# A graph network's sorted messages: ScalarE places the kept edge ends at fixed places, VectorE's selection steps read them without register loads

## The reference

```python
x = x + L0_gnn(layernorm(x), edge_index, edge_attr, u, batch, W1, b1, W2, b2)   # mean of edge_attr by src, two-layer MLP
x = x + L0_ffn(layernorm(x)[None], ...)[0]                                      # two experts of eight, GELU, layer norm
x = x + L1_gnn(layernorm(x), W, edge_index)
x = x + L1_ffn(layernorm(x)[None], ...)[0]                                      # one expert per token, capacity 977

def L1_gnn(x, W, edge_index):
    src, dst = edge_index
    h = x @ W
    deg = segment_sum(ones_like(dst), dst)
    deg_inv_sqrt = where(deg > 0, rsqrt(maximum(deg, 1)), 0.0)
    norm = deg_inv_sqrt[src] * deg_inv_sqrt[dst]
    return segment_sum(h[src] * norm[:, None], dst)
```

## Time and profile before

| what | value |
|---|---|
| median of 3 runs | 3174.09 us (3173.44 to 3176.77) |
| the profiled execution | 3175.92 us, its span 3174.1 us |
| TensorE (PE) | 2284.6 us busy, 72% |
| VectorE (DVE) | 2044.1 us busy, 64% |
| GpSimd (POOL) | 2067.8 us busy, 65% |
| ScalarE (ACT) | 863.4 us busy, 27% |
| granted TensorE clock, mean | 0.826 |
| the chain that ended last | PE 35%, POOL 25%, issue 15%, DVE 13% |

### The profile page before, as it was taken

How to read it: one execution, slowest core, us unless ns; L and a number is a source line. 1 busy time by engine, 2 the same in 40 slices (tenths; PEclk the granted TensorE clock), 3 DMA queues, 4 the chain that set the end, 5 groups by cost and what they waited for, 6 DMA issues and landing times.

```text
span 3174.1 us, 49123 instructions
## 1 busy us (share of the span) xinstructions
PE 2284.6 (72%) x14349; PEld 2096.1 (66%) x14350; DVE 2044.1 (64%) x3305; ACT 863.4 (27%) x2246; POOL 2067.8 (65%) x1707
## 2 busy tenths in 40 slices
PE   0000047779899995997889984777887877798997
PEld 0000036668888885775889873666676767798997
DVE  8889976732323332465788876765665567488987
ACT  0000012210000000132545442344454421354543
POOL 5777877777777775010555545567788742488886
PEclk9999998865555555698999996899999895699999
DMA  6543345455444452122011114566777753423231
GB/s 202 151 115 94 81 124 152 146 163 123 114 114 117 113 136 71 50 77 66 20 49 51 51 61 139 140 165 187 193 197 190 192 146 112 86 63 84 63 90 33
DMA packets 341517, 358.60 MB, mean 113 GB/s; under 512 B 209280, under 2 KB 248560, under 8 KB 341125
## 3 DMA queue, kind: packets, MB, share of 16 engines
q1 hardware_dynamic: 209538, 196.84, 21.3%
q0 software_dynamic: 105984, 93.52, 13.0%
q10 hardware_dynamic: 25853, 66.46, 6.8%
HBM read 234.90 MB, written 122.85 MB: 113 GB/s over the span
## 4 chain that ended last, share of the span: by engine, by line
PE 35%; POOL 25%; issue 15%; DVE 13%; DMA 4%; DVEq 4%; SPq 4%; ACT 1%; another core or an unknown queue 0%; POOLq 0%; ACTq 0%
POOL sorted L989 18%; PE ps L1984 13%; PE ps L2133 4%; POOL h_lo L1028 3%; PE ps L2033 3%; PE ps L2152 3%; PE ps L2143 3%; DVEq L1596 2%; DVE hT L1606 2%; DVE yb L1874 2%; PE ps L2011 2%; POOL rstd L998 1%; SPq L595 1%; SPq L594 1%; DMA big<-x_rows,idx_a 1%
## 5 line engine op out<-in xcount | busy, mean ns | idle before, releaser
L1064 POOL DMA_INDIRECT mid<-h_rows,idx_a x400 | 485.5, 1214 | 172.5 <-issue 113.7
L1984 PE MATMUL ps<-big 128*128 128x65 f32 x2380 | 528.6, 419 | 87.5 <-issue 49.7
L1984 PEld LDWEIGHTS ps<-big 128*128 128x128 f32 x2380 | 514.0, 331 | 103.2 <-issue 102.4
L1361 DVE COPY mid<-big 128x28 f32 (+1 forms) x85 | 22.6, 266 | 448.2 <-PE ps L1984 306.8
L998 POOL TENSOR_TENSOR rstd<-var,neg_half 125x2 f32<-125x2 f32 (+1 forms) x75 | 63.2, 843 | 373.1 <-DVE var L1413 373.0
L989 POOL DMA_INDIRECT sorted<-yb,idx_a x200 | 239.6, 1198 | 83.9 <-issue 60.5
L989 POOL DMA_INDIRECT sorted<-wk,idx_a x200 | 238.1, 1191 | 60.9 <-issue 60.9
L989 POOL DMA_INDIRECT sorted<-xh,idx_b x200 | 237.9, 1190 | 60.9 <-issue 60.6
L989 POOL DMA_INDIRECT sorted<-mid,idx_b x200 | 237.9, 1190 | 60.9 <-issue 60.3
L2152 PE MATMUL ps<-adj,h_in_r 128*128 128x304 f32 (+3 forms) x980 | 244.2, 376 | 38.3 <-issue 36.1
L1606 DVE TENSOR_TENSOR hT<-ps,mid 128x608 bf16<-128x608 f32 (+3 forms) x245 | 255.1, 1041 | 0.1
(11 more groups left out here) (333 smaller groups left out, 6534.4 us busy)
## 6 DMA issues: line engine op xcount, KB each, us to landing
h_in_r<-h_parts SPq DMA_DIRECT2D x245, 256.0 KB
big<-sorted ACTq DMA_DIRECT2D x85, 469.0 KB
sorted<-hT SPq DMA_DIRECT2D x73, 469.0 KB
mid<-in_L_ffn_w SPq DMA_DIRECT2D x16, 1024.0 KB
hid_x<-hT ACTq DMA_DIRECT2D x25, 500.0 KB
mid<-hid_x SPq DMA_DIRECT2D x25, 500.0 KB
h_parts<-h_part_r SPq DMA_DIRECT2D x25, 500.0 KB
mid<-h_rows,idx_a POOLq DMA_INDIRECT x400
```

The costliest lines, as they stand in the source:

```text
L1064: nc.gpsimd.indirect_dma_start(mg4[:, s, i, :], None, h_rows, bass.IndirectOffsetOnAxis(idx4[:, s, i:i + 1], 0)).then_inc(s_gk[s], 16)
L1984: i_ = mm(banks[:, bass.ds(o_, CW)], node_hot[:, s % 2, i, :], rows2[:, s, i, 0:CW], start=False, stop=True, skip_group_check=True)
```

## The change

ScalarE gets new work during the sort. For each of the five dense chunks it copies the kept ends of each of the 49 buckets from `keep` to a fixed place in a new buffer `kept` (539 columns, twice). It does this in pieces of 8 buckets (the last piece of a chunk 9), one piece behind each low column of blocks 50 to 79. Each piece is a hardware loop with one register load and one copy in its body, and it waits first until VectorE's copy into `keep` has come far enough. SP's write to device memory now waits for the 245 placed copies instead of the bucket means. VectorE writes the tile at which each bucket starts as integers in `positions` already (`first_words`), and copies only the first 48 groups into `keep`.

In the messages the steps then have fixed places. All the target offsets are added ahead of the first step, six adds over whole tables, which end in `dst_rel`. A step has one comparison of low sources over all its tiles, one comparison of targets, and no register load.

```diff
+NK = 48
+STEP_TILES = tuple(sum(CAPS[c] for c in chunks) for _, chunks, _ in RANGES)
+KEPT_AT = tuple(TB * sum(STEP_TILES[:r]) for r in range(len(RANGES) - 1)) + (TB * sum(STEP_TILES[:len(RANGES) - 2]),)
+REL_AT = tuple(TB * sum(STEP_TILES[:r]) for r in range(len(RANGES)))
+KS = TB * sum(STEP_TILES[:-1])
+KEEP_AT = (50, 56, 62, 68, 74)
+KEEP_PARTS = ((0, 8), (8, 16), (16, 24), (24, 32), (32, 40), (40, 49))
...
-            sp.wait_ge(s_a0, 1)
-            sp.dma_start(sorted_ends, keep[:, :, 0:KD]).then_inc(s_endk, 16)
+            sp.wait_ge(s_kset, ND * TB)
+            sp.dma_start(sorted_ends, kept).then_inc(s_endk, 16)
...
+            def place_kept(c, part):
+                r = FIRST_OF_RANGE[c]
+                o_ = sum(CAPS[k] for k in RANGES[r][1] if k < c)
+                to = kept[:, :, KEPT_AT[r]:KEPT_AT[r] + TB * STEP_TILES[r]].rearrange("p c (h k) -> p c h k", h=TB)
+                act.wait_ge(s_keep, sum(CG[:c + 1]) + 1)
+                with act.Fori(*KEEP_PARTS[part]) as h:
+                    first = act.value_load(first_words[0:1, bass.ds(c * TB + h, 1)], min_val=0, max_val=KD - CAPS[c])
...
+                    act.activation(to[:, :, bass.ds(h, 1), o_:o_ + CAPS[c]].rearrange("p c a k -> p c (a k)"), keep[:, :, bass.ds(first, CAPS[c])], ACT.Copy).then_inc(s_kset, 1)
...
             for b in blocks:
                 low_column(b)
+                for c in range(ND):
+                    if 0 <= b - KEEP_AT[c] < len(KEEP_PARTS):
+                        place_kept(c, b - KEEP_AT[c])
                 for _ in range(2 + b % 2):
...
+                    v.tensor_scalar(first_words[:, c * TB:(c + 1) * TB], ps[0:1, 4, 128:128 + TB], float(GFIRST[c] * GA), None, ALU.add).then_inc(s_dve, st.up())
...
-                v.tensor_copy(keep[:, :, bass.ds(g * GA, GA)], rows2[:, s, :, CW:RW].rearrange("p t c -> p c t"))
+                if kept:
+                    v.tensor_copy(keep[:, :, bass.ds(g * GA, GA)], rows2[:, s, :, CW:RW].rearrange("p t c -> p c t")).then_inc(s_keep, 1)
...
             def select_edges(r, h, q, i):
...
-                o_, firsts = 0, []
-                for c in chunks:
-                    first = dve.value_load(first_words[0:1, bass.ds(c * TB + h, 1)], min_val=0, max_val=KD - CAPS[c])
...
-                    v.tensor_tensor(dst_rel[:, s, o_:o_ + CAPS[c]], kept_dst[:, bass.ds(first, CAPS[c])],
-                                    to_rel[MADD.index((r, c))][:, bass.ds(h, 1), :].rearrange("p a t -> p (a t)"), ALU.add).then_inc(s_rel, 1)
-                    firsts.append((o_, first, CAPS[c]))
-                    o_ += CAPS[c]
-                for o_, first, k in firsts:
-                    v.tensor_tensor(node_sel[:, s, o_:o_ + k, :], near[:, 0:BR].unsqueeze(1).to_broadcast([BR, k, BR]),
-                                    kept_lo[:, bass.ds(first, k)].unsqueeze(2).to_broadcast([BR, k, BR]), ALU.is_equal)
-                dve.wait_ge(s_rel, REL + RELS[r] + (q - r * TB + 1) * len(chunks) + 12 * len(chunks) * i)
+                v.tensor_tensor(node_sel[:, s, 0:n, :], near[:, 0:BR].unsqueeze(1).to_broadcast([BR, n, BR]),
+                                kept_lo[:, bass.ds(h * n + KEPT_AT[r], n)].unsqueeze(2).to_broadcast([BR, n, BR]), ALU.is_equal)
                 v.tensor_tensor(dst_sel[:, s, 0:n * w].rearrange("p (k w) -> p k w", w=w), near[:, 0:w].unsqueeze(1).to_broadcast([BR, n, w]),
-                                dst_rel[:, s, 0:n].unsqueeze(2).to_broadcast([BR, n, w]), ALU.is_equal).then_inc(s_dsel2, 1)
+                                dst_rel[:, bass.ds(h * n + REL_AT[r], n)].unsqueeze(2).to_broadcast([BR, n, w]), ALU.is_equal).then_inc(s_dsel2, 1)
...
+                for k, (r, c) in enumerate(MADD):
+                    o_ = sum(CAPS[j] for j in RANGES[r][1] if j < c)
+                    n = STEP_TILES[r]
+                    v.tensor_tensor(dst_rel[:, REL_AT[r]:REL_AT[r] + TB * n].rearrange("p (h k) -> p h k", h=TB)[:, :, o_:o_ + CAPS[c]],
+                                    kept_dst[:, KEPT_AT[r]:KEPT_AT[r] + TB * n].rearrange("p (h k) -> p h k", h=TB)[:, :, o_:o_ + CAPS[c]],
+                                    to_rel[k], ALU.add).then_inc(s_tabs, sorted_.up())
```

More of the change, by code:

```diff
@@ L42 @@
 NB = NODES + 128
+FIRST_OF_RANGE = tuple(min(r for r in range(len(RANGES)) if c in RANGES[r][1]) for c in range(ND))
 MADD = tuple((r, c) for r in range(len(RANGES)) for c in RANGES[r][1])
@@ L270, in build @@
         agg = mid[0:BR, 0:TB * DE].rearrange("p (t d) -> p t d", t=TB)
-        keep = mid[0:BR, 3200:3200 + 2 * KT].rearrange("p (c t) -> p c t", c=2)
+        keep, o = cut(mid, BR, 3200, 2 * GA * NK)
+        keep = keep.rearrange("p (c t) -> p c t", c=2)
+        kept, o = cut(mid, BR, o, 2 * KS)
+        kept = kept.rearrange("p (c t) -> p c t", c=2)
+        assert o <= 5850
         wA1e = mid[0:DE, 5850:5850 + HID0]
@@ L309, in build @@
         node_sel = node_sel.bitcast(bf16).rearrange("p (s t q) -> p s t q", s=2, t=5)
-        dst_rel, o = cut(mid, BR, o, 2 * 5)
-        dst_rel = dst_rel.rearrange("p (s t) -> p s t", s=2)
+        dst_rel, o = cut(mid, BR, o, TB * sum(STEP_TILES))
         less_base, o = cut(mid, BR, o, len(RANGES) + 1)
@@ L387, in build @@
         s_const = sem("constants_set")
+        s_keep, s_kset = sem("sorted_ends_copied"), sem("sorted_ends_placed")
         s_rawT = sem("ends_transposed")
@@ L707, in load_sorted @@
                 act.dma_start(rows2[:, s], sorted_v[c][:, j * GA:(j + 1) * GA, :]).then_inc(s_srow[s], 16)
+            def place_kept(c, part):
[5 more added lines that the diff above has]
+                    first = act.value_load(first_words[0:1, bass.ds(c * TB + h, 1)], min_val=0, max_val=KD - CAPS[c])
+                    first = nc.s_assert_within(first, 0, KD - CAPS[c], skip_runtime_bounds_check_because="a bucket starts at a tile of its chunk")
+                    act.activation(to[:, :, bass.ds(h, 1), o_:o_ + CAPS[c]].rearrange("p c a k -> p c (a k)"), keep[:, :, bass.ds(first, CAPS[c])], ACT.Copy).then_inc(s_kset, 1)
             groups = list(range(NGA))
@@ L1353, in _, with sorted_hot @@
             v.tensor_scalar(deg[:, :], cnt[:, :], 1.0, None, ALU.max).then_inc(s_deg, 1)
-            def sorted_hot(g, s=None):
+            def sorted_hot(g, s=None, kept=True):
                 s = g % NS if s is None else s
@@ L1585, in add_range @@
                 dve.wait_ge(s_radd, RADD + r + 1)
-            RELS = tuple(TB * sum(len(RANGES[k][1]) for k in range(r)) for r in range(len(RANGES)))
             def select_edges(r, h, q, i):
-                w, chunks, _ = RANGES[r]
-                s, n = q % 2, sum(CAPS[c] for c in chunks)
+                w, n = RANGES[r][0], STEP_TILES[r]
+                s = q % 2
                 if not (isinstance(i, int) and q + 12 * i < 2):
                     dve.wait_ge(s_adj, ADJ + q + 12 * i - 1)
-                o_, firsts = 0, []
-                for c in chunks:
-                    first = dve.value_load(first_words[0:1, bass.ds(c * TB + h, 1)], min_val=0, max_val=KD - CAPS[c])
-                    first = nc.s_assert_within(first, 0, KD - CAPS[c], skip_runtime_bounds_check_because="a bucket starts at a tile of its chunk")
-                    v.tensor_tensor(dst_rel[:, s, o_:o_ + CAPS[c]], kept_dst[:, bass.ds(first, CAPS[c])],
-                                    to_rel[MADD.index((r, c))][:, bass.ds(h, 1), :].rearrange("p a t -> p (a t)"), ALU.add).then_inc(s_rel, 1)
-                    firsts.append((o_, first, CAPS[c]))
-                    o_ += CAPS[c]
-                for o_, first, k in firsts:
-                    v.tensor_tensor(node_sel[:, s, o_:o_ + k, :], near[:, 0:BR].unsqueeze(1).to_broadcast([BR, k, BR]),
-                                    kept_lo[:, bass.ds(first, k)].unsqueeze(2).to_broadcast([BR, k, BR]), ALU.is_equal)
-                dve.wait_ge(s_rel, REL + RELS[r] + (q - r * TB + 1) * len(chunks) + 12 * len(chunks) * i)
+                v.tensor_tensor(node_sel[:, s, 0:n, :], near[:, 0:BR].unsqueeze(1).to_broadcast([BR, n, BR]),
+                                kept_lo[:, bass.ds(h * n + KEPT_AT[r], n)].unsqueeze(2).to_broadcast([BR, n, BR]), ALU.is_equal)
                 v.tensor_tensor(dst_sel[:, s, 0:n * w].rearrange("p (k w) -> p k w", w=w), near[:, 0:w].unsqueeze(1).to_broadcast([BR, n, w]),
-                                dst_rel[:, s, 0:n].unsqueeze(2).to_broadcast([BR, n, w]), ALU.is_equal).then_inc(s_dsel2, 1)
+                                dst_rel[:, bass.ds(h * n + REL_AT[r], n)].unsqueeze(2).to_broadcast([BR, n, w]), ALU.is_equal).then_inc(s_dsel2, 1)
             def select_turn(r, i):
```

19 lines of the change are left out of this document (10 added, 9 removed).

## The result

The changed kernel takes **3137.93 us** (median of 4 runs, 3134.15 to 3142.72) against 3175.43 for the kernel before beside it (4 runs): ratio 0.9884, 95% interval 0.9866 to 0.9901, 37 us faster. Two later sets of runs gave 3139.75 (ratio 0.9887) and 3142.72 (0.9895). The forecast was 3139. In one kernel further down (the equality done again in the first range, beside the mark) one of ten executions took 4205.61 us and is left out. The profiled execution took 3142.72, its span is 3140.8 us (before 3174.1), so its own difference is 33.3.

What follows compares the result with a forecast made beforehand. The prediction took POOL's 400 gathers (606.5 us) as the bound, with 37.4 us of waiting to win: -34.4 waiting, -1 reload, 0 placing make -35.4, from the median 3174.09 to 3139 us; own range 3135 to 3147, wider 3133 to 3154.

Steps and rivals of the forecast that it cites:

- The third step: Dearest of three VectorE bucket steps in a first-range turn, from TensorE's adjacency to window add: 4.03 to 2.39 us, 1.64 saved.
- A turn of 8.2 us: First range, window add to window add: down from 10.15 us, chosen between 8.5 and 7.7, with VectorE's floor at 7.13.
- 3 us of waiting remain: Gather stage: of POOL's 37.4 us true waiting 3 stay, put at the range change, so -34.4 us (bounds -37.4 to -21).
- the 10 us of lead for POOL: First range: first turn's copies end near 1946, POOL needs window 3 at 1956.2; at 8.2 us a turn 9.3 is used.
- Reload -1: Before the first gather: reloads of the kept columns shrink from 647 to 539 columns, saving 1 us (0 to 1.7).
- Setup even: Before the first step: six table adds (1.2 us) replace a cast and two register loads (1.6 us); POOL doesn't see it.
- Placing, x = 1.2 and cost 0: ScalarE's loops in the sort: 1.2 us a bucket (0.8 to 1.4), hidden in its sleep; cost 0 (0 to +13 us).
- The formula for larger x: Sort, blocks 72 to 75: placing costs 32x - 38.5 us, x being ScalarE's us per bucket; 6 at 1.4, 13 at 1.6.
- B: Rival: ScalarE's placing loop is somewhat dear, 1.6 us a bucket, adding 13 us: 3152 us; chance 0.08.
- C: Rival: placing above 1.9 us a bucket, ScalarE falls behind from block 50 on; 91 us at 2.2, 3230 us; chance 0.06.
- A: Rival: TensorE, not VectorE, holds the first range; turn 9.1 us, 16 us of waiting remain, 3152 us; chance 0.11.
- D: Rival: the placing only trades, with POOL's index copies late for another cause; 3172 us; chance 0.03.

Runs made afterwards that it cites:

- the mark: The changed kernel with no edit, run again beside three follow-up kernels on a chip where the kernel before takes 3175.19 us: 3142.72 us, ratio 0.9895.
- the doubled equality: The changed kernel with two more 3-tile low-source equalities in each first-range step, written to unused room: 3177.57 us, ratio 1.0007; earlier, on the slower chip, 3268.41 us.
- the placing alone: ScalarE's placing as in the changed kernel but read by nothing, with the message steps of the kernel before: 3174.22 us, ratio 1.0003.
- the loads back: The changed kernel with VectorE's register loads put back in every step, values unused: 3161.19 us, ratio 0.9949; earlier, on the slower chip, 3266.49 us.
- the early indices: The changed kernel with ScalarE waiting only for the edge ends' own reload before making the first gather indices: 3139.24 us, ratio 0.9895.
- the kernels that place twice: The changed kernel with each placed load and copy made twice, the second into unused room: 3272.47 us on the slower chip, 3161.31 us on the other.

## Why the prediction was right

- **POOL's gathers set the stage, and 37.4 us of its waiting are all there is to win: right.** True waiting is 0.7 us after, first to last gather went down by 37.9 (forecast 34.4), and the doubled equality brings 34.9 back.
- **The third step, 4.03 to 2.39 us: right** (1971.75 to 1974.04 is 2.29; the equality of five tiles 816 ns for 798 forecast). What made it dear was shown one by one: without loads but with adds and split equality a turn is 7.77, with loads alone 8.85, with both 10.14. Against the mark's mean of 7.32 the two together cost 0.8 us a turn more than the sum of each alone; that rest isn't explained.
- **A turn of 8.2 us: mis-sized, 7.15 measured.** The term was read off today's TensorE row and moved half way. TensorE gave all of it back, since its pair and window sum had been long at the lower clock level (granted 0.81 before from 1940 to 2060 us, 0.95 to 0.98 in three profiles of the changed kernel). I had worked out 7.13 as VectorE's floor, and that is what stands. How clock and turn go together is seen in the runs (0.76 at 10.16, 0.81 at 10.15, 0.84 at 8.85, 0.98 at 7.32); which moves the other in the loads' run is not shown.
- **3 us of waiting remain: mis-sized, 0.7, and its working was wrong in a way that the short turn hid.** The wrong term is the 10 us of lead for POOL. The forecast had the first turn's copies end near 1946; the trace of before has four adjacency copies there (the range's extra step is among them), and the index copy behind them at 1950.65. A gather follows its index copy by 1.17 us (1979.14 to 1980.31), so window 3, wanted at 1956.3, had 4.5 us of lead:

```profile
1950.65 0.20 ACT L831 ACTIVATE idx_a<-ends 125x5 uint32<-125x5 f32 x1
1980.31 1.21 POOL L1064 DMA_INDIRECT mid<-h_rows,idx_a  x1 [1.51 <-ACT idx_a L831]
2112.71 0.20 ACT L831 ACTIVATE idx_a<-ends 125x5 uint32<-125x5 f32 x1
```

  The next 15 index copies lie 10.05 us apart, which is 37.1 us more than POOL wants, and the one over the range change (2101.46 to 2112.71) is 3.7 us longer than 7.58. So 37.1 + 3.7 - 4.5 = 36.3 of the 37.4 us. The same sum gives 37.1 for the placing alone (37.8 measured), 35.9 for the doubled equality (36.6) and 17.6 with the loads back (18.2); some 0.65 stands in every profile, the changed kernel's too. The forecast's 3 us for the range change was about right (0.8 to 4.9 in these). In the changed kernel the lead is 6.9 us. By this sum 6 to 9 us, not 3, would have remained at a turn of 8.2, an estimate from these copies. That the remainder came out small is luck: the turn was taken too long and the lead too large, and the two cancel.
- **Reload -1: the first gather came 1.3 us earlier, but not by that cause.** The reload shrank by 0.35 us, and taking its wait away moved the first gather by 0.2 to 0.3 us, counted from POOL's last work before it. In the placing alone, where the reload is as long as before (9.42), the first gather starts earlier still, at 1929.0.
- **Setup even: right in the result.** It never reached POOL; the three groups of table work end at 1936.5, and the first index copies don't depend on them.
- **Placing, x = 1.2 and cost 0: right.** x is 1.07 us (1.04 in an undisturbed piece), chunk 6's first load was at 1139.64 for 1143 forecast, and the placing alone has a ratio of 1.0003. The bound from below, 0.8, was too low: the turn of the loop is 0.83 us of idle plus a copy of 0.208. The 0.1 for the dynamic destination rested on no row; the copy's address work takes 0.109 (0.074 and 0.035). The formula for larger x stood its one test (18.8 for 20.7), which also speaks for the slope behind rivals B and C. Their condition is refuted: B needed 1.6 us, C 1.9. All this holds for chips of this kind: on the one where the kernel before takes 3262 us, POOL waits for low columns in the sort (31.7 and 29.9 us with the loads back, 24 times), the forecast's sign of being wrong. What makes them late there, the placing or something else, isn't shown. "DMA: Bandwidth & Descriptors" of the Trainium skill (Latency and other measured facts) gives a register load a floor of about 600 ns; ScalarE's 245 loads have a median of 282, so the trace doesn't agree.
- **Rivals A and D:** TensorE doesn't hold the first range (it rests 1.18 us a turn), and the gain is where the waits were. The gathers last 1211 ns beside a VectorE that is busy all the time. The rule of "SBUF" in the Trainium skill (SBUF: two separate sides), by which a VectorE operation that holds the shared ports keeps POOL from writing descriptors, had no share here. It may not be tested at all: the page names operations in a two-port mode or with two inputs from SBUF, and the equalities take one of their two inputs from PSUM (`ps`).
- **The sum:** -35.4 forecast, -33.3 in the profiled execution, -37.5, -35.4 and -32.5 in the medians of three sets. In the profile the gather stage gave 3.5 us more than forecast and the last stage, which has the same code, took 6.7 more (411.6 for 404.9). That the median lands within 2 us is luck beside such a spread. Over the profiles on these chips the last stage takes 402.7 to 411.6 us. The three kernels with turns of 10.15 have 404.9, 405.8 and 406.4, and six of the seven others 407.8 to 411.6, so that a longer last stage behind a faster first range isn't excluded; the early indices, with 402.7, speak against it. Why it varies is open.

## What to carry to other kernels

Find the engine whose rate can't be undercut (here 400 x 1.516 us), count its true waits by taking the ordinary gaps off its idle time, and take those as the ceiling of any gain upstream. A register load in a step is cheap only while it runs ahead: behind a semaphore wait two of them took 1.37 us, of which 0.80 stood in the path, so indices that are fixed per step are worth precomputing on an engine that sleeps. Here the granted clock came up from 0.81 to 0.95 or more once the feeding engine no longer paused, and the turn fell to the feeder's own floor (7.15), not to a value between old and new (8.2); so work that floor out as a bound of its own. And count a lead from the copy that is really the first, with the extra step in it.

## What the runs showed of the hardware

- A hardware loop on ScalarE with one register load and one small copy with dynamic places takes 1.04 us a turn (load 0.282, copy 0.208); a second load and copy in the body add 0.7.
- 20 matmuls of the window sum take 2.37 us at a granted clock of 1.00, 3.91 at 0.59 (in the doubled equality, after a rest of 1.91 us ahead of its pair) and 4.47 at 0.51 (in the one long turn of the changed kernel).
- Two register loads on VectorE behind a wait take 1.37 us to the operation that follows (loads back, 1977.82 to 1979.19).
- On the chip where the kernel before takes 3262 us the gathers last the same 1211 ns, but simple register operations stall now and then. By line, the first row is of the loads-back kernel on that chip, the second of the same kernel on the other:

```profile
L725 ACTq FUSED_REGOPS  x245: 3/152/711, 763.0 to 1280.6; - x123
```

```profile
L725 ACTq FUSED_REGOPS  x245: 152/152/173, 741.2 to 1197.6; - x123
```

  The idle time before the 245 copies is 266.6 us there and 213.3 here, and the first gather starts 71 us later (2002.0 for 1930.8). The gather stage is longer there with the loads (661.5 us for 622.2) and without them (631.2 for 605.5, in the kernels that place twice). What makes the difference between the chips is open.
